# Second attention's loop: the next products are summed at the head of a step, the turns are spread over two steps

## The chip, the cores and the metric

One core of a Trainium2 chip runs the whole program in one launch. The metric is the device time of one execution in microseconds (us), lower is better. The kernel before takes 2010.0 us, the median of three runs.

## The reference, cut to what matters

Two layers, each an attention and a mixture of experts, over x of 8 x 512 tokens with 256 features. Only the second layer's attention, and what is loaded for the experts behind it, is touched.

```python
qkvw = x @ w_qkvw                      # x: 8 x 512 x 256
# sliced into q, k, v, w; 32 "batches" of 16 heads, head size 4, and the
# softmax runs over 16 heads' worth of positions, 16 x 16 scores at a time
attn = softmax(q @ k.T * 4 ** -0.5)
o = (attn @ v) * w @ w_out
x = x + gate * o
# then: layernorm, router (8 experts, the best one), gelu(x @ W1[e]) @ W2[e]
```

## The kernel before, in words

The program is written out by hand for five engines, each with its own list of instructions; semaphores are the only order between the lists, and each engine works strictly through its own list. All large tiles lie in one buffer, BIG, so the profile shows that name for nearly all of them.

The second attention runs as a loop of 64 steps q = 0 to 63; eight steps make a chunk c = q // 8. Step q of each engine's list:

- **GpSimd** (`products`, `values`): two products of q and k for step q + 2, into one of two buffers PB (128x1024, L1959); then half of the weighted values of step q (128x512, L1959), which waits for the exponentials of step q (`e_sb`). At steps 8c + 1 and 8c + 2 one pass of `finish` for the chunk before (128x1024).
- **VectorE** (`top`, `values`, `sums`): the maximum of the scores of step q + 1 (L1542), the weighted values of step q (L1111), the sums of step q - 1 (L1564), at every second step moments of an output tile (L1118), at the end of a chunk a reciprocal (L1567).
- **ScalarE** (`powers`, `powers_beside`): the exponentials of step q + 1 (L1880), copies of what TensorE projected or turned (L1618), the exponentials once more, into BIG (L1887), which sets `e_sb`.
- **TensorE**: `less_max(q + 1)` (waits for VectorE's maximum), at odd steps `out_project`, then the projections of a later chunk's heads (`project`, 16 for each chunk), the turns of its q and k (`turn_qk`, four for each chunk, each of four small transposing groups), at even steps `out_less`, then `scores(q + 2)`, which sums GpSimd's products (waits for `pm`), and at odd steps `out_turn`. The output tiles run in steps 13 to 61.

The heads of chunk c are projected in seven steps from 8c - 10 on (3, 3, 2, 2, 2, 2, 2), those of chunk 1 in steps 0 to 3 (4 each). All four turns of the next chunk stand in step 8c + 5. GpSimd can't start the products of a chunk before the four turned tiles are copied out of PSUM (`qt`).

SyncE's list issues the loads. The weights of the second layer's experts come in as 32 pieces of 512 KB (`weights_in(1, i)`, L499) whenever the part of BIG that they take is free: 4 behind chunk 4, 5 behind chunk 5, 6 after the last scores, 17 (`late`) later. Of these 15 are issued with every second of the rows that `rows_out` stores behind the loop, from row 3 on, and 2 after the last. `rows_out` stores each normalised row tile to HB (128 KB, L508) from a ring of four buffers; ScalarE waits for a store's landing before it fills the buffer again. TensorE reads the first piece only when all 32 have landed.

The router's weights are split into a high part (ScalarE) and a low part (VectorE) at tick 2 of that phase (`pre_tick`).

Of the kernel before, what the change touches and what calls it, by code (L numbers as in the profile page):

```python
# [8 lines left out]
ALU = mybir.AluOpType  # L9
# [59 lines left out]
def program(nc, x_in, wqk_in, wv_in, wo_in, rw_in, rb_in, w1_in, w3_in, w2_in, c0_in, m0_in,  # L69
# [3 lines left out]
    with ctx:  # L73
# [222 lines left out]
        def at(l, n):  # L296
            return per_layer[n] if l else 0
# [66 lines left out]
        def heads_by_step(c):  # L364
            if c == 1:
                return {0: 4, 1: 4, 2: 4, 3: 4}
            return {8 * c - 10 + n: k for n, k in enumerate((3, 3, 2, 2, 2, 2, 2))}

        heads_at = {q: [] for q in range(-10, 8 * 8)}
        for c in range(1, 8):  # L370
# [4 lines left out]

        def turns_next(q):

            return range(4) if q % 8 == 5 and q < 56 else ()

        NQ = 64  # L380
        N_IN = 24
# [51 lines left out]
        def sync(e):  # L433
# [136 lines left out]
            def out_weights_in(c):  # L570
                if c >= 6:
                    sp.wait_ge(s["pj_ps"], 128)
                elif c >= 2:
                    sp.wait_ge(s["pd_ps"], 4 * (c - 2) + 4)
                e.dma_start(out_weights(c).rearrange("p m k d -> p (m k d)"), WB[c]).then_inc(ld_wu[c % 2], 16)

            for c in range(7):
                heads_out(c)
                out_weights_in(c)
                for n in range(4 * c, 4 * c + 4):  # L580
                    out_in(n)
                if c == 1:
                    router_in(1)
                if c == 4:

                    sp.wait_ge(s["pj_ps"], 64)
                    for i in range(4):
                        weights_in(1, i)
                if c == 5:

                    sp.wait_ge(s["rl_ps"], 32)
                    sp.wait_ge(s["pj_ps"], 128)
                    sp.wait_ge(s["pm"], pm_p[55])
                    for i in (4, 5, 16, 17, 29):
                        weights_in(1, i)
            out_weights_in(7)
            sp.wait_ge(s["s_ps"], NQ)
            sp.wait_ge(s["pm"], pm_p[NQ - 1])
            for i in (12, 13, 14, 15, 19, 20):
# [7 lines left out]
            sp.wait_ge(s["mx_ps"], NQ)  # L607
            sp.wait_ge(s["pd_ps"], N_IN)
            sp.wait_ge(s["fin"], 16)
            late = [6, 7, 8, 9, 10, 11, 18, 21, 22, 23, 24, 25, 26, 27, 28, 30, 31]  # L610
            for n in range(3, NT):
                rows_out(1, n)
                if n % 2:
                    weights_in(1, late.pop(0))
            for i in late:
                weights_in(1, i)
# [13 lines left out]
        def tensor(e):  # L630
# [376 lines left out]
            def scores(q):  # L1007
                if q >= NQ:
                    return
                if pm_by(q).count("d"):  # L1010
                    pe.wait_ge(s["pm_d"], pm_v[q])
                pe.wait_ge(s["pm"], pm_p[q])
                if q >= 3:
                    pe.wait_ge(s["e_sb"], q - 2)
                else:
                    pe.wait_ge(s["cb_m"], NT)
                    pe.wait_ge(s["seld"], 4)
                for b in range(4):
                    m = mm(ps[2 + q % 3][32 * b:32 * b + 32, :], seld, PB[q % 2][:, b].rearrange("p r f -> p (r f)"), True, False)
                m.then_inc(s["s_ps"], 1)  # L1020

            def less_max(q):
                if q >= NQ:
                    return
                pe.wait_ge(s["sm"], q + 1)
                mm(shaped(ps[2 + q % 3][:, :], (2, 16, 16)), negid, bc(SM[q % 4], 3, 16), False, True).then_inc(s["mx_ps"], 1)
# [42 lines left out]
            less_max(0)  # L1069
            scores(1)  # L1070
            for q in range(NQ):
                less_max(q + 1)
                for n in out_at(q, O_OUT):
                    out_project(n)
                for c, h in heads_at[q]:
                    project(c, h)
                turn_qk(q // 8 + 1, turns_next(q))
                for n in out_at(q, O_LESS):
                    out_less(n)
                scores(q + 2)  # L1080
                for n in out_at(q, O_TURN):
                    out_turn(n)
            pe.wait_ge(s["e_sb"], NQ)
# [23 lines left out]
        def vector(e):  # L1107
            dve = Lane(e)

            def tt(o, a, b, op):  # L1110
                return e.tensor_tensor(o, a, b, op)  # L1111
# [167 lines left out]
            attended(NT - 1)  # L1279


            def pre_tick(l, t):
                m_ = M[l]
                for k, i in steps(NT, 7, t):
                    if k != 0:
                        continue
                    b = i // 4
                    if i == 2:
                        dve.wait_ge(s["rw_hi"], at(l, "rw_hi") + 1)
                        tt(m_.RW[1].rearrange(FLAT), m_.RWf.rearrange(FLAT), m_.RW[0].rearrange(FLAT), ALU.subtract).then_inc(s["rw_lo"], 1)  # L1290
                    o = at(l, "hr")
                    if l:
                        dve.wait_ge(s["rs_v"], (52, 54, 56)[max(b - 5, 0)])
                    else:
                        dve.wait_ge(s["rs_v"], 16 + 2 * b + 2)
                    dve.wait_ge(s["sc_ps"], at(l, "sc_ps") + b + 1)
                    if i >= 4:
                        dve.wait_ge(s["hs_lo"], at(l, "hs_lo") + i - 3)
                    h, sc = m_.HR[i % 4], ps[4 + b % 2]
                    x = row_tile(l, i)  # L1300
                    e.scalar_tensor_tensor(out=h, in0=X[:, x, :], scalar=stat[:, x, 0:1], in1=sc[:, 256:512],
                                           op0=ALU.subtract, op1=ALU.mult).then_inc(s["hr"], 1)
                    dve.wait_ge(s["hr"], o + 2 * i + 1)
                    e.scalar_tensor_tensor(out=h, in0=h, scalar=rstd[:, x:x + 1], in1=sc[:, 0:256],
                                           op0=ALU.mult, op1=ALU.add).then_inc(s["hr"], 1)
# [249 lines left out]
            def sums(q):  # L1555
                if q < 0:
                    return
                c, q2 = q // 8, q % 8
                dve.wait_ge(s["vm"], vm_n[q])
                dve.wait_ge(s["vm_p"], q + 1)  # L1560
                dve.wait_ge(s["e_sb"], q + 1)
                if q2 == 0 and c >= 2:
                    dve.wait_ge(s["fin"], 2 * (c - 2) + 1)
                e.tensor_reduce(OB[c % 2][:, 2 * q2:2 * q2 + 2], PV[q % 2], AX.X, ALU.add).then_inc(s["vr"], 1)  # L1564
                if q2 == 7:
                    dve.wait_ge(s["vr"], q + 1)
                    e.reciprocal(OB[c % 2][:, :, :, 4], OB[c % 2][:, :, :, 4]).then_inc(s["rcp"], 1)  # L1567

            def out_measure(n):
                dve.wait_ge(s["wx"], n + 1)  # L1570
                moments(3 * NT + n, out_tile(n))
# [4 lines left out]
            for q in range(NQ):  # L1576
                top(q + 1)
                values(q, 0)
                values(q, 1)
                sums(q - 1)  # L1580
                for n in out_at(q, O_MEASURE):
                    out_measure(n)
            sums(NQ - 1)

            def deviation(g):
# [28 lines left out]
        def scalar(e):  # L1614
# [104 lines left out]
            root(15, row(NT - 1))  # L1719


            def pre_tick(l, t):
                m_ = M[l]
                for k, i in steps(NT, 7, t):
                    if k == 5:
                        act.wait_ge(s["hT_ps"], at(l, "hT_ps") + i + 1)
                        if i >= 2:
                            act.wait_ge(s["lg_ps"], at(l, "lg_ps") + i - 1)
                        copy(m_.HTR[i % 2], bank16(6 + i % 2)).then_inc(s["hT"], 1)
                    if k == 2:  # L1730
                        act.wait_ge(s["hr"], at(l, "hr") + 2 * i + 2)
                        if i >= 4:
                            act.wait_ge(st_hb[i % 4], slot_base[l]["hb"] + 16 * (i // 4))
                            act.wait_ge(s["hT_ps"], at(l, "hT_ps") + i - 3)
                        copy(m_.HP[i % 4][:, 0, :], m_.HR[i % 4]).then_inc(s["hs_hi"], 1)
                    if k == 0 and i == 2:
                        act.wait_ge(ld_r, slot_base[l]["r"] + 32)
                        copy(m_.RW[0].rearrange(FLAT), m_.RWf.rearrange(FLAT)).then_inc(s["rw_hi"], 1)

            def routing(l):  # L1740
                m_ = M[l]
# [168 lines left out]
            for q in range(NQ):  # L1910
                powers(q + 1)
                for n in out_at(q, O_OUT):
                    out_x(n)
                for n in out_at(q - 1, O_TURN):
                    out_hi(n)
                for c, h in heads_at[q]:
                    project(c, h)
                turn_qk(q // 8 + 1, turns_next(q))
                for n in out_at(q, O_LESS):
                    out_lo(n)  # L1920
                powers_beside(q + 1)

            def late_root(g):
# [271 lines left out]
```

## Time and profile before

| | |
|---|---|
| median of three runs | 2010.0 us (2005.67 to 2013.35) |
| the profiled execution | 2012.52 us, its span 2010.4 us |
| mean granted TensorE clock | 0.893 of full |
| loop of the second attention | about 1211 to 1639 us of the span |
| rows stored, routing | about 1639 to 1712 us |
| experts and the end | about 1712 to 2010 us |
| busy share of the span | TensorE 85%, VectorE 57%, GpSimd 52%, ScalarE 43% |

A row of the timeline gives the start and length in us of one instruction, or of several in a row of one kind (x26: 26 of them), with the time that the engine was idle before it and the work that released it. GpSimd is POOL, VectorE DVE, ScalarE ACT, TensorE PE (its weight loads PEld), SyncE SP. The clock column of a stretch is the granted clock as a share of 2.4 GHz. An idle engine matters only where it is the one that others wait for.

### The profile page before, as it was taken

The page shows a single profiled execution, that of the slowest core. Times are in us where ns is not written, and L with a number is a line of the kernel's source. Part 1 is how long each engine was busy: PE and PEld are TensorE (multiplying, and loading weights), DVE is VectorE, ACT ScalarE, POOL GpSimd, SP SyncE. Part 2 cuts the span into 40 slices and gives each one's busy share as a digit, 9 for nine tenths or more (in the row PEclk, how much of TensorE's full clock was granted, in tenths as well). Part 3 has the DMA queues.
Part 4 walks back from the last instruction along what each step waited for, and adds up shares of the span by engine and source line. Part 5 has one row for each costly group of instructions (what it writes and reads, how often), then busy time and mean ns, then how long its engine had stood idle before and what let it go on. Part 6 is the DMA issues. An engine that isn't in the chain of part 4 may idle for free.

```text
span 2010.4 us, 32271 instructions
## 1 busy us (share of the span) xinstructions
PE 1715.6 (85%) x11144; PEld 1040.9 (52%) x11144; DVE 1141.3 (57%) x1837; ACT 866.5 (43%) x1940; POOL 1047.0 (52%) x861
## 2 busy tenths in 40 slices
PE   5699999977899999999999367788887766899993
PEld 3355555554466666666666232334333234577771
DVE  6798898866232332332333685888888886212124
ACT  3444444334344444444444374344444335444443
POOL 3377777623233333333443697989888853233322
PEclk8699999975899999999999678899889876899996
DMA  5013332007322332222443510011102147111115
GB/s 210 1 42 105 105 105 99 28 32 281 107 82 84 93 95 92 90 79 88 129 137 85 165 43 1 22 27 27 27 25 69 65 138 235 35 43 43 43 39 174
DMA packets 114358, 170.47 MB, mean 85 GB/s; under 512 B 27920, under 2 KB 78112, under 8 KB 114080
## 3 DMA queue, kind: packets, MB, share of 16 engines
q1 hardware_dynamic: 104032, 140.61, 20.6%
q0 software_dynamic: 10176, 27.80, 5.3%
q8 instruction: 102, 1.67, 0.4%
q14 instruction: 48, 0.39, 0.1%
HBM read 105.19 MB, written 63.18 MB: 84 GB/s over the span
## 4 chain that ended last, share of the span: by engine, by line
PE 69%; DVE 19%; issue 3%; DMA 3%; ACT 3%; POOL 2%; SPq 0%; DVEq 0%; POOLq 0%; ACTq 0%
PE ps L634 62%; DVE BIG L1111 8%; PE ps L905 5%; DVE BIG L1564 4%; ACT BIG L1618 1%; PE ps L877 1%; DVE bnst L1118 1%; DVE BIG L1542 1%; DMA BIG<-YT 1%; DVE X L1111 1%; POOL BIG L2072 1%; PE ps L809 1%; PE ps L749 1%; DMA HB<-BIG 1%; POOL X L1959 1%
## 5 line engine op out<-in xcount | busy, mean ns | idle before, releaser
L634 PE MATMUL ps<-BIG 128*128 (+8 forms) x8100 | 1318.0, 340 | 150.8 <-DVE BIG L1542 78.3
L634 PEld LDWEIGHTS ps<-BIG 128*128 128x128 f16 (+2 forms) x8100 | 746.2, 105 | 633.8 <-issue 137.4
L1959 POOL TENSOR_TENSOR BIG<-BIG 128x512 f16<-128x512 f32 (+4 forms) x528 | 763.1, 1474 | 309.7 <-ACT BIG L1618 287.7
L1618 ACT ACTIVATE BIG<-ps 128x512 f16<-128x512 f32 (+5 forms) x1036 | 397.6, 441 | 518.6 <-PE ps L634 270.6
L1111 DVE TENSOR_TENSOR BIG<-ps,BIG 128x512 f32<-128x512 f32 (+4 forms) x693 | 460.8, 718 | 272.8 <-ACT BIG L1618 225.8
L2046 POOL DMA_INDIRECT YT<-BIG x106 | 105.1, 992 | 542.2 <-ACT BIG L1618 542.2
L1111 DVE TENSOR_TENSOR BIG<-BIG,ps 128x512 f32<-128x512 f32 (+1 forms) x204 | 120.9, 597 | 413.6 <-PE ps L634 398.4
L1618 ACT ACTIVATE BIG<-BIG 128x512 f16<-128x512 f32 (+2 forms) x329 | 200.4, 626 | 130.7 <-DVE BIG L1111 98.8
L1769 ACT ACTIVATE BIG<-ps 128x512 f32<-128x512 f32 x212 | 126.8, 598 | 135.7 <-PE ps L634 135.7
L1564 DVE TENSOR_REDUCE BIG<-BIG 128x160 f32<-128x2560 f32 x64 | 180.8, 2826 | 0.0
L2041 POOL DMA_INDIRECT BIG<-HB,BIG x106 | 103.2, 973 | 69.8 <-DVE BIG L1111 43.8
L905 PE MATMUL ps<-ident,BIG 128*128 128x128 f32 x848 | 109.9, 273 | 0.0
L905 PEld LDWEIGHTS ps<-ident,BIG 128*128 128x128 f32 x848 | 99.2, 141 | 20.1
L1880 ACT ACTIVATE ps<-ps 128x512 f32<-128x512 f32 x64 | 37.2, 582 | 137.6 <-PE ps L634 137.6
L1111 DVE TENSOR_TENSOR BIG<-BIG 128x1024 f32<-128x1024 f32 (+16 forms) x115 | 80.9, 727 | 17.6 <-ACT BIG L1618 14.3
L1542 DVE TENSOR_REDUCE BIG<-ps 128x32 f32<-128x512 f32 x64 | 43.7, 682 | 79.3 <-PE ps L634 79.3
L634 PE MATMUL ps<-MOD,sel 8*128 8x256 f32 (+1 forms) x96 | 55.8, 703 | 27.5 <-DVE BIG L1111 15.7
L634 PE MATMUL ps<-BIG,tri 128*128 128x512 f16 x260 | 64.2, 389 | 5.1 <-DVE BIG L1111 5.1
L1118 DVE BATCH_NORM_STATS2 bnst<-X 128x6 f32<-128x256 f32 x128 | 53.9, 421 | 8.0 <-DMA X<-in_x 3.3
L1887 ACT ACTIVATE BIG<-ps 128x512 f32<-128x512 f32 x64 | 38.5, 602 | 37.9 <-DVE BIG L1564 37.8
L877 PEld LDWEIGHTS ps<-ident,BIG 128*128 128x128 f16 x424 | 32.7, 99 | 36.8 <-issue 12.4
L877 PE MATMUL ps<-ident,BIG 128*128 128x128 f16 x424 | 41.6, 221 | 11.1 <-DMA BIG<-HB,BIG 11.1
(128 smaller groups left out, 864.7 us busy)
## 6 DMA issues: line engine op xcount, KB each, us to landing
WD<-BIG SPq DMA_DIRECT2D x112, 256.0 KB, 2.3
BIG<-in_v SPq DMA_DIRECT2D x32, 512.0 KB, 5.1
BIG<-WD SPq DMA_DIRECT2D x32, 512.0 KB, 5.1
BIG<-in_w SPq DMA_DIRECT2D x24, 512.0 KB, 3.9
BIG<-WD SPq DMA_DIRECT2D x32, 384.0 KB, 7.5
BIG<-YT SPq DMA_DIRECT2D x24, 512.0 KB, 4.8
HB<-BIG SPq DMA_DIRECT2D x64, 128.0 KB, 3.0
X<-in_x SPq DMA_DIRECT2D x4, 1024.0 KB, 12.1
```

Source lines behind the costliest of these rows:

```text
L634: return e.matmul(o, lhsT, rhs, start=start, stop=stop, skip_group_check=True)
L877: m = e.transpose(bank16(6 + idx % 2)[:, k, :], m_.HIN[j % 3][:, k * 128:(k + 1) * 128], ident16[:, :])
L905: m = e.transpose(ps[6 + (2 + 3 * j + q) % 2][:, n * 128:(n + 1) * 128], m_.UP[j % 2][:, (4 * q + n) * 128:(4 * q + n + 1) * 128], ident[: ...
L1111: return e.tensor_tensor(o, a, b, op)
L1118: e.bn_stats(bnst[:, r, :], X[:, i, :]).then_inc(s["bn"], 1)
L1542: e.tensor_reduce(SM[q % 4], shaped(ps[2 + q % 3][:, :], (2, 16, 16)), AX.X, ALU.max).then_inc(s["sm"], 1)
L1564: e.tensor_reduce(OB[c % 2][:, 2 * q2:2 * q2 + 2], PV[q % 2], AX.X, ALU.add).then_inc(s["vr"], 1)
L1618: return e.activation(o, i, ACT.Copy)
L1769: e.activation(m_.UP[j % 2][:, hf * 512:hf * 512 + 512], ps[idx % 4][:, :], ACT.Silu if m_.gated else ACT.Gelu).then_inc(s["su"], 1)
L1959: return e.tensor_tensor(o, a, b, op)
L2041: e.indirect_dma_start(m_.HIN[j % 3], None, m_.HB, bass.IndirectOffsetOnAxis(m_.gi[:, j:j + 1], 0)).then_inc(ld_hi[j % 3], 16)
L2046: e.indirect_dma_start(m_.YT, bass.IndirectOffsetOnAxis(m_.yi[:, j:j + 1], 0), m_.YO[j % 2], None).then_inc(st_y[j % 2], 16)
```

## The change

- `scores(q + 2)` moves from behind `out_less` to the head of TensorE's step q, ahead of `less_max(q + 1)`.
- The heads of a chunk are projected in six steps instead of seven (3, 3, 3, 3, 2, 2), and the four turns are spread over steps 8c + 4 (two) and 8c + 5 (two).
- Pieces 8 and 11 of the second layer's expert weights are issued behind chunk 5, pieces 6 and 9 before the last scores; `late` holds 13 pieces, and one is issued with every fourth row instead of every second (8 with rows, 5 after the last).
- The router's weights of the second layer are split inside the loop: the high part at ScalarE's step 40, the low part at VectorE's step 42.

```diff
         def heads_by_step(c):
             if c == 1:
                 return {0: 4, 1: 4, 2: 4, 3: 4}
-            return {8 * c - 10 + n: k for n, k in enumerate((3, 3, 2, 2, 2, 2, 2))}
+            return {8 * c - 10 + n: k for n, k in enumerate((3, 3, 3, 3, 2, 2))}
...
         def turns_next(q):
-            return range(4) if q % 8 == 5 and q < 56 else ()
+            return {4: (0, 1), 5: (2, 3)}.get(q % 8, ()) if q < 56 else ()
...
                     sp.wait_ge(s["pm"], pm_p[55])
-                    for i in (4, 5, 16, 17, 29):
+                    sp.wait_ge(s["fin"], 12)
+                    for i in (4, 5, 16, 17, 29, 8, 11):
                         weights_in(1, i)
             out_weights_in(7)
+            sp.wait_ge(s["vm"], vm_n[55])
+            sp.wait_ge(s["vm_p"], 56)
+            for i in (6, 9):
+                weights_in(1, i)
...
-            late = [6, 7, 8, 9, 10, 11, 18, 21, 22, 23, 24, 25, 26, 27, 28, 30, 31]
+            late = [7, 10, 18, 21, 22, 23, 24, 25, 26, 27, 28, 30, 31]
             for n in range(3, NT):
                 rows_out(1, n)
-                if n % 2:
+                if n % 4 == 3:
                     weights_in(1, late.pop(0))
...
             for q in range(NQ):
+                scores(q + 2)
                 less_max(q + 1)
                 for n in out_at(q, O_OUT):
                     out_project(n)
...
                 for n in out_at(q, O_LESS):
                     out_less(n)
-                scores(q + 2)
                 for n in out_at(q, O_TURN):
                     out_turn(n)
...
+            def router_lo(l):
+                m_ = M[l]
+                dve.wait_ge(s["rw_hi"], at(l, "rw_hi") + 1)
+                tt(m_.RW[1].rearrange(FLAT), m_.RWf.rearrange(FLAT), m_.RW[0].rearrange(FLAT), ALU.subtract).then_inc(s["rw_lo"], 1)
...
                     out_measure(n)
+                if q == 42:
+                    router_lo(1)
...
+            def router_hi(l):
+                act.wait_ge(ld_r, slot_base[l]["r"] + 32)
+                copy(M[l].RW[0].rearrange(FLAT), M[l].RWf.rearrange(FLAT)).then_inc(s["rw_hi"], 1)
...
                     out_lo(n)
+                if q == 40:
+                    router_hi(1)
                 powers_beside(q + 1)
```

## Rows read from the trace of the kernel before

**Rows 1.** The page: shares of the chain that ended last, by engine.
```profile
PE 69%; DVE 19%; issue 3%; DMA 3%; ACT 3%; POOL 2%; SPq 0%; DVEq 0%; POOLq 0%; ACTq 0%
```

**Rows 2.** Busy time of two stretches of eight steps (us, instructions, TensorE's clock, DMA).
```profile
1255.70:1304.80 49.10, 37.05 (x209) 14.52 (x209) 42.67 (x34) 19.73 (x68) 45.91 (x27) 0.88 0.09 22
1358.40:1413.00 54.60, 44.26 (x261) 20.94 (x262) 44.75 (x41) 23.15 (x81) 46.28 (x27) 0.91 0.10 25
```

**Rows 3.** Waits in steps 6 to 61: total us, times, longest.
```profile
DVE BIG L1542 <- PE ps L634: 61.8, 27, 5.1
POOL BIG L1959 <- ACT BIG L1618: 48.2, 7, 8.3
...
POOL BIG L1959 <- ACT BIG L1887: 8.2, 9, 2.4
```

**Rows 4.** Timeline of GpSimd: start, us, work, idle before it and its releaser.
```profile
1254.48 45.90 POOL L1959 TENSOR_TENSOR BIG<-BIG 128x1024 f32<-128x1024 f32 x26 [6.31 <-ACT BIG L1618]
...
1303.57 26.49 POOL L1959 TENSOR_TENSOR BIG<-BIG 128x1024 f32<-128x1024 f32 x15 [3.19 <-ACT BIG L1618]
...
1395.23 7.22 POOL L1959 TENSOR_TENSOR BIG<-BIG 128x1024 f32<-128x1024 f32 x4
1402.92 1.28 POOL L1959 TENSOR_TENSOR BIG<-BIG 128x512 f32<-128x512 f32 x1 [0.47 <-ACT BIG L1887]
...
1412.05 26.51 POOL L1959 TENSOR_TENSOR BIG<-BIG 128x1024 f32<-128x1024 f32 x15 [7.84 <-ACT BIG L1618]
1439.13 17.88 POOL L1959 TENSOR_TENSOR BIG<-BIG 128x512 f32<-128x512 f32 x10 [0.57 <-ACT BIG L1887]
...
1576.24 46.57 POOL L1959 TENSOR_TENSOR BIG<-BIG 128x1024 f32<-128x1024 f32 x26 [7.97 <-ACT BIG L1618]
```

**Rows 5.** Timeline of step 29, the turns of four.
```profile
1402.68 0.67 DVE L1542 TENSOR_REDUCE BIG<-ps 128x32 f32<-128x512 f32 x1
...
1403.41 1.78 PE L634 MATMUL ps<-BIG 128*128 128x512 f32 x8 [2.05 <-DVE BIG L1542]
...
1405.55 2.40 PE L634 MATMUL ps<-BIG,ident 32*32 32x512 f32 x16
...
1407.83 1.24 ACT L1618 ACTIVATE BIG<-ps 128x512 f32<-128x512 f32 x2 [1.58 <-PE ps L634]
```

**Rows 6.** Timeline of steps 30 and 31, three heads each.
```profile
1413.78 3.32 PE L634 MATMUL ps<-BIG 128*128 128x512 f32 x20 [0.18 <-DVE BIG L1542]
...
1417.14 1.06 PE L634 MATMUL ps<-BIG 128*32 128x512 f32 x8
...
1419.37 1.78 PE L634 MATMUL ps<-BIG 128*128 128x512 f32 x8 [1.17 <-DVE BIG L1542]
...
1424.09 0.62 ACT L1887 ACTIVATE BIG<-ps 128x512 f32<-128x512 f32 x1
```

**Rows 7.** Busy time and clock of short stretches, after waits of various length.
```profile
1273.30:1279.80 6.50, 6.40 (x22) 2.52 (x22) 4.42 (x4) 2.09 (x8) 6.50 (x5) 0.52 0.01 4
1280.50:1284.00 3.50, 3.43 (x22) 1.63 (x22) 3.50 (x3) 1.60 (x7) 3.50 (x3) 1.00 0.00 0
...
1378.20:1382.00 3.80, 3.80 (x11) 1.94 (x12) 3.80 (x3) 0.58 (x1) 3.80 (x3) 0.55 0.00 0
```

**Rows 8.** Timeline: the last maximum of the loop.
```profile
1625.31 0.69 DVE L1542 TENSOR_REDUCE BIG<-ps 128x32 f32<-128x512 f32 x1 [1.11 <-PE ps L634]
```

**Rows 9.** Waits behind the loop, ScalarE's for the row buffers.
```profile
ACT BIG L1618 <- DMA HB<-BIG: 5.2, 5, 1.4
```

**Rows 10.** Busy time while the last rows are stored.
```profile
1680.00:1694.40 14.40, 10.76 (x118) 6.84 (x118) 6.61 (x15) 9.66 (x22) 7.67 (x15) 0.50 0.95 312
```

**Rows 11.** Timeline of SyncE's queue: pieces of the weights.
```profile
1589.31 2.29 SPq L499 DMA_DIRECT2D BIG<-WD  x5
...
1693.48 1.47 SPq L499 DMA_DIRECT2D BIG<-WD  x3
```

**Rows 12.** Chain of waits: the first products with those weights.
```profile
1717.33 5.32 PE ps L634 x12
```

More of the change, by code:

```diff
@@ L1287, in pre_tick @@
                     b = i // 4
-                    if i == 2:
-                        dve.wait_ge(s["rw_hi"], at(l, "rw_hi") + 1)
-                        tt(m_.RW[1].rearrange(FLAT), m_.RWf.rearrange(FLAT), m_.RW[0].rearrange(FLAT), ALU.subtract).then_inc(s["rw_lo"], 1)
+                    if l == 0 and i == 2:
+                        router_lo(0)
                     o = at(l, "hr")
@@ L1735, in pre_tick @@
                         copy(m_.HP[i % 4][:, 0, :], m_.HR[i % 4]).then_inc(s["hs_hi"], 1)
-                    if k == 0 and i == 2:
-                        act.wait_ge(ld_r, slot_base[l]["r"] + 32)
-                        copy(m_.RW[0].rearrange(FLAT), m_.RWf.rearrange(FLAT)).then_inc(s["rw_hi"], 1)
+                    if l == 0 and k == 0 and i == 2:
+                        router_hi(0)
             def routing(l):
```

## The prediction

> **What bounds the kernel now.** I read the page's chain first: it ends on TensorE for 69% and on VectorE for 19% [rows 1]. That is an average over stages, so I cut the second attention's loop into its eight-step chunks. There no engine is full: in 54.6 us TensorE is busy 44.3, VectorE 44.8, GpSimd 46.3 [rows 2]. The waits say that VectorE stands 61.8 us for TensorE's sums before a maximum, and GpSimd 48.2 us, seven times, for ScalarE [rows 3]. The first is what the move of `scores` would take away. The second decides how much of it can be kept. GpSimd's timeline shows it working 45.9 us without a gap, 26 instructions, the work of a chunk, and then standing 3.2 to 8 us for the turned tiles; outside that it waits only 0.47 and 0.57 us [rows 4]. So a chunk lasts 45.9 us plus GpSimd's idle time: 46.57 + 7.97 = 54.5, for instance. However early the maxima come, time is gained only where GpSimd idles less. Its price by piece, from the same rows: two products 4.0 us, values 1.25, so a step takes it 5.25 us.
>
> **The turn, before and after.** Let t = 0 be the end of GpSimd's last products of a chunk, 1395.23 + 7.22 = 1402.45. Before, the next products start at 1412.05, 9.6 us later [rows 4], because the turns wait for `less_max` and `out_project` (1403.41 to 1405.55, 2.14 us) and are then four [rows 5]. After the change TensorE at step 8c + 5 must first sum the very products that end at t = 0: 1.06 us [rows 6], 1.2 with issue. Then 2.14 for `less_max` and `out_project`, then two turns: 2.28 from their start to the first copy (1405.55 to 1407.83) and 1.24 for two copies [rows 5]. That is 6.9, GpSimd starts at 7.0: **2.6 us less** for a chunk. The other two turns stand in step 8c + 4, which has no heads any more: 1.2 + 0.55 + 2.4 + 0.3 = 4.5 us against GpSimd's 5.25, hidden.
>
> **What it gives back.** The moved sum is a new wait: TensorE stops at the head of step 8c + 6 until the first products of the new chunk are there, at 7.0 + 4.0 = 11.0, while it was free at 1.2 + 2.14 + 2.4 + 0.7 = 6.45. Behind that wait stand `less_max(8c + 7)`, three heads and, through ScalarE's copies, the second exponentials for which GpSimd's values wait. It is 4.5 us idle, and rows show the clock after such waits at 0.52 and 0.55, the 1.2 GHz level; the same 22 matmuls then took 6.40 instead of 3.43 us, the other stretch cost 3.8 x 0.45 = 1.7 us of work [rows 7]. I take 2.3 us, between 1.7 and 3.0, and bound it below by none. Step 8c + 6 then takes 1.06 + 3.36 [rows 6] + 2.3 = 6.6, to 17.6, with copies and exponentials to 18.5. GpSimd is ready at 11.0 + 1.25 + 4.0 = 16.25: it waits **2.25 us** (0 at full clock, 3 at most).
>
> In step 8c + 7, odd with three heads, the exponentials start 4.72 us after `less_max` starts (1419.37 to 1424.09 [rows 6]) and last 0.6; with the sum ahead of them they are done 6.5 us after the products, where GpSimd comes back after 5.25. Counted from 17.9 they end at 24.3, GpSimd is ready at 23.8: **0.5 us**, and 1.3 to 1.5 if step 8c + 6 ran at full clock. In step 8c + 11 (two heads, 0.8 less) it is 5.7 against 5.25: **0.5 us**. In steps 8c + 9 and 8c + 10 `finish` gives GpSimd 2 us of other work, which covers them. Sum 3.25 us; the 0.47 and 0.57 of before go. Per chunk: -2.6 + 3.25 - 1.04 = **-0.4 us** (from -2.0 at full clock to +0.8), five chunks: **-2.0 us**.
>
> **The other chunks.** The turn in step 5: GpSimd idled 6.31 us before 1254.48. The new way to the turned tiles has no `out_project`, 1.2 + 0.55 + 3.5 = 5.3 us after its products, 2.8 us earlier. But in steps 0 to 3, with four heads, the second exponentials come 1.2 + 0.55 + 3.3 + 0.9 = 5.95 us after the products, 0.6 to 0.7 late, in about two steps. Net **-1.7**. The turn in step 13: idle before 3.19 [rows 4], after 5.4 - 1.25 = 4.1, and then the 2.25 of the low clock: **+3.2** (from +0.9). The last chunk has no turn behind it and no heads: from the products at 1576.24 eight pairs, seven values and two passes of `finish`, 32 + 8.8 + 4 = 44.8, and 1.2 to the last maximum, against 1625.31 - 1576.24 = 49.07 before [rows 4, 8]: **-3.0**. The loop: -1.7 + 3.2 - 2.0 - 3.0 = **-3.5 us**.
>
> **The weights and the router.** Behind the loop ScalarE waits 5.2 us in all for the ring's stores to land [rows 9], at a DMA share of 0.95 while the last rows go out [rows 10]. Half of the pieces among the rows are gone. I take 2.3 of the 5.2 us, as part of the waits lies beside TensorE's late output tiles; bounds 0 and 5.2. Now five pieces instead of three are issued at the end, near 1694 [rows 11]. At the 312 GB/s of that stretch five are 8.5 us, landed near 1703; the weights are first used at 1717.3 [rows 12], so they cost nothing, and would from 14 us more. The four pieces moved into the loop go where SyncE stood still anyway: 8 and 11 behind the five at 1589 [rows 11], ahead of a store of the heads that GpSimd hasn't finished by then; 6 and 9 behind that store. Their new waits (`fin` 12, `vm`, `vm_p` of step 55) ask for what the stores of the heads before them in SyncE's list have already waited for, so nothing queues up behind them. The router's two small instructions fill gaps on VectorE and ScalarE in the loop: -0.2 behind it. Tail **-2.5 us**.
>
> **Sum.** -3.5 - 2.5 = -6.0 us on the profiled execution, 2012.5 to 2006.5. That execution lies 2.5 above the median of the runs, 2010.0, so the forecast is **2004 us**.
>
> **Rivals.** (C) *GpSimd's waits outside the turn vanish*, because the clock holds and the steps after a turn fit beside 5.25 us. Then a chunk is 45.9 + 5.7 = 51.6, so -3.6 x 5 = -18; with -1.7 + 0.9 - 3.0 and -3 in the tail -25 us, 1985. For it: TensorE has only 44 us of work in a chunk, some of it at low clock; against it the odd steps with three heads, 6.5 us. (B) *All is given back*: 4.3 us of waits in a chunk and a tail limited by TensorE's late tiles. -2.6 + 4.3 - 1.04 = +0.66 a chunk, +3.3 for five in place of -2.0, tail -0.2: +1.6, about 2011.5. (D) *Slower: step 8c + 7 runs at the low clock too.* Its 5.5 us become 5.5 x 1.87 = 10.3 (the ratio of 6.40 to 3.43 [rows 7]), 4.8 us more wait of GpSimd in each of five chunks, +24: 2028. It decides from 3.2 us a chunk on. Against it: the stretch behind the low one, after a wait of only 0.8 us, is back at 1.00. The Trainium skill ("TensorE: Matmul & The Clock Gate", section "Why this matters for your kernels") has a rule against this change: waiting gaps between bursts of matmuls put the clock back to its lower level. Taken for step 8c + 6 alone it gives the forecast, taken for every waiting step it gives D. The rows agree for the long waits, not for those of 0.8 us.
>
> **Chances.** The forecast (about 1999 to 2008) 0.50, B 0.20, C 0.17, D 0.13. What a measurement here can tell from no change is about 0.5%, 10 us. Faster by more: C and a third of the forecast's band, 0.33. Slower by more: D and the edge of B, 0.16. The rest 0.51. The range from 1989 to 2016 takes in the low clock from none to full on step 8c + 6, a tail from 0 to 5.2 and half of C, and leaves out D and C's far end.
>
> **What would show it.** VectorE's 61.8 us of waits for sums shrink or move to other places, and TensorE waits for GpSimd at the heads, about 4.5 us once in a chunk. GpSimd's waits before new products fall from 7.9 to about 5.7 us, and new ones of 1 to 3 us for L1887 appear in the two steps after. A low clock stands behind each such wait. Chunks of 54 to 54.5 us confirm the sum, of 52 C, of 58 D. The prediction is wrong if GpSimd is no longer the fullest engine of a chunk, or if stores to HB still hold ScalarE for 5 us.

## The result: slower by 0.9%, and the profile after

The changed kernel takes 2027.6 us, the median of five runs (2026.08 to 2031.96), against 2010.2 of the kernel before, measured with it: a ratio of 1.0088 with an interval of 1.0068 to 1.0108. The forecast was 2004, with a range up to 2016; the measurement lies outside it. The profiled execution took 2026.8 us, its span 2024.7, 14.3 more than before. In the changed kernel's rows VectorE's maximum is L1551, its weighted values L1116, GpSimd's products and values L1975, ScalarE's two exponentials L1894 and L1901, its copies L1629, TensorE L639.

The page, the shares of the chain by engine, as [rows 1]:

```profile
PE 63%; POOL 14%; DVE 10%; issue 6%; DMA 3%; ACT 3%; SPq 0%; POOLq 0%; DVEq 0%; ACTq 0%
```

Before, the chain ended on TensorE and VectorE, with 2% for GpSimd; now GpSimd holds 14% of it and VectorE 10%. A chunk of eight steps, as [rows 2] (length, busy us of TensorE, its weight loads, VectorE, ScalarE, GpSimd, the clock, DMA):

```profile
1358.10:1416.30 58.20, 44.44 (x260) 20.60 (x260) 45.47 (x42) 22.58 (x81) 46.08 (x27) 0.88 0.10 24
```

The work is the same, 44.4 us of TensorE and 46.1 of GpSimd, and the chunk lasts 58.2 us where it lasted 54.6. The waits in the same stretch, from the first turn to the last maximum (total us, times, longest), as [rows 3]:

```profile
PE ps L639 <- POOL BIG L1975: 94.2, 41, 4.6
DVE BIG L1551 <- PE ps L639: 42.8, 15, 4.7
POOL BIG L1975 <- ACT BIG L1901: 38.3, 21, 3.2
DVE BIG L1116 <- ACT ps L1894: 37.1, 27, 1.9
...
POOL BIG L1975 <- ACT BIG L1629: 29.7, 6, 5.7
```

VectorE's wait for sums fell from 61.8 to 42.8 us, but 37.1 us of waits for the first exponentials appeared behind it. TensorE, which waited 1.2 us for GpSimd before, does it 41 times, 94.2 us. GpSimd's wait for the turned tiles is 29.7 us in six turns here; with the turn of step 5, whose 3.46 us lie just ahead of this stretch, it is 33.1 in seven, against 48.2 in seven before. Its wait for the second exponentials rose from 8.2 to 38.3: what the turns gave is more than given back. Where, GpSimd's timeline shows, as [rows 4]: the start of a chunk in steps 6 and 14, one whole chunk (steps 30 to 37), and the last one.

```profile
1248.65 9.11 POOL L1975 TENSOR_TENSOR BIG<-BIG 128x1024 f32<-128x1024 f32 x5 [3.46 <-ACT BIG L1629]
...
1301.50 9.12 POOL L1975 TENSOR_TENSOR BIG<-BIG 128x1024 f32<-128x1024 f32 x5 [2.47 <-ACT BIG L1629]
...
1416.27 9.11 POOL L1975 TENSOR_TENSOR BIG<-BIG 128x1024 f32<-128x1024 f32 x5 [5.24 <-ACT BIG L1629]
1428.18 10.39 POOL L1975 TENSOR_TENSOR BIG<-BIG 128x512 f32<-128x512 f32 x6 [2.80 <-ACT BIG L1901]
1439.15 19.73 POOL L1975 TENSOR_TENSOR BIG<-BIG 128x512 f32<-128x512 f32 x11 [0.58 <-ACT BIG L1901]
1462.03 6.70 POOL L1975 TENSOR_TENSOR BIG<-BIG 128x512 f32<-128x512 f32 x4 [3.14 <-ACT BIG L1901]
1474.13 2.00 POOL L1975 TENSOR_TENSOR BIG<-BIG 128x1024 f32<-128x1024 f32 x1 [5.39 <-ACT BIG L1629]
...
1590.27 9.11 POOL L1975 TENSOR_TENSOR BIG<-BIG 128x1024 f32<-128x1024 f32 x5 [5.41 <-ACT BIG L1629]
```

From the first products of a chunk to the next: 52.85 us for the one with the turn of step 13 (49.09 before), then 56.6, 58.2, 57.9, 58.5 and 57.7, where it was 54.5, 54.0, 54.7, 55.0 and 54.5. The five together are 16.1 us longer. In the chunk shown GpSimd idles 5.24 us for the turns, 2.80 behind step 8c + 6, 0.58, and **3.14 us at 1462.03**, behind step 8c + 11 (here 35), where the forecast had 0.5. The critical chain through this place (start, length, work; x3: three instructions):

```profile
1447.45 6.30 POOL BIG L1975 x3
1453.75 0.04 issue
1453.79 7.14 PE ps L639 x30
...
1461.46 0.50 ACT BIG L1901
1461.96 0.07 issue
1462.03 0.95 POOL BIG L1975
```

Read it forward. GpSimd's products for TensorE's head of step 35 end at 1453.75. TensorE sums them at once and works through the step for 7.14 us; only then come ScalarE's second exponentials, and GpSimd's next values start at 1462.03. TensorE's own rows at the heads of steps 34 and 35, and the clock of four stretches, as [rows 7]: step 30's head, step 34, the wait after it, step 35.

```profile
1446.29 3.43 PE L639 MATMUL ps<-BIG 128*32 128x512 f32 x22 [1.93 <-POOL BIG L1975]
...
1453.79 5.22 PE L639 MATMUL ps<-BIG 128*32 128x512 f32 x16 [3.96 <-POOL BIG L1975]
```

```profile
1420.30:1426.80 6.50, 6.50 (x29) 2.80 (x29) 2.62 (x4) 1.89 (x8) 5.08 (x3) 0.63 0.00 0
1446.30:1449.70 3.40, 3.40 (x23) 1.72 (x23) 2.40 (x5) 1.25 (x5) 3.40 (x2) 1.00 0.00 0
1449.90:1453.70 3.80, 0.00 (x0) 0.00 (x0) 3.72 (x3) 1.14 (x5) 3.80 (x3) 0.83 0.76 155
1453.80:1459.00 5.20, 5.20 (x17) 2.01 (x18) 1.31 (x2) 0.58 (x1) 5.09 (x3) 0.50 0.19 60
```

Step 34 is over in 3.4 us at the full clock. Then TensorE does nothing for 3.96 us, and the first 5.2 us of step 35 run at 0.50, the 1.2 GHz level; its last 2.3 us show 0.95. The 6.5 us at 0.63 at 1420.3 are the low stretch that was forecast; the one at 1453.8 was not. The same happens in the last chunk (TensorE's last sum, and, as [rows 8], the last maximum):

```profile
1637.07 4.22 PE L639 MATMUL ps<-BIG 128*32 128x512 f32 x16 [1.70 <-POOL BIG L1975]
```

```profile
1639.58 0.68 DVE L1551 TENSOR_REDUCE BIG<-ps 128x32 f32<-128x512 f32 x1
```

Sixteen matmuls take 4.22 us there, and 2.78 us at the full clock elsewhere; the last maximum starts 49.31 us after the chunk's first products (1639.58 minus 1590.27), against 49.07 before. Behind the loop ScalarE's waits for the row buffers went from 5.2 to 4.4 us, as [rows 9]:

```profile
ACT BIG L1629 <- DMA HB<-BIG: 4.4, 4, 2.4
```

So the 14.3 us are: -5.8 up to the first chunk's products (1254.48 to 1248.65; 1.75 of them were already there before the loop, where the code is the same), +3.8 for the chunk of step 13, +16.1 for five chunks, +0.2 for the last, +1.1 from the last maximum to `finish` and -1.1 from there to the end.

### The profile page after: what moved, and what is told of

It reads as the page before. It is cut to its first block, busy times and chain, and to the rows that moved or that the text cites. A ratio compares the mean times of both kernels' runs of the same rounds, so it can differ in the third digit from the quotient of the medians.

```text
span 2024.7 us, 32272 instructions
## 1 busy us (share of the span) xinstructions
PE 1710.4 (84%) x11144; PEld 1034.7 (51%) x11144; DVE 1143.0 (56%) x1837; ACT 862.9 (43%) x1940; POOL 1048.9 (52%) x861
## 4 chain that ended last, share of the span: by engine, by line
PE 63%; POOL 14%; DVE 10%; issue 6%; DMA 3%; ACT 3%; SPq 0%; POOLq 0%; DVEq 0%; ACTq 0%
PE ps L639 56%; POOL BIG L1975 13%; DVE BIG L1116 5%; PE ps L910 5%; ACT BIG L1629 1%; PE ps L882 1%; DMA BIG<-YT 1%; POOL BIG L2088 1%; DVE X L1116 1%; DMA HB<-BIG 1%; DVE bnst L1123 1%; POOL X L1975 1%; PE ps L814 1%; PE ps L754 1%; DMA BIG<-in_m 0%
## 5 line engine op out<-in xcount | busy, mean ns | idle before, releaser
L639 PE MATMUL ps<-BIG 128*128 (+9 forms) x8100 | 1320.6, 342 | 175.0 <-POOL BIG L1975 114.2
L639 PEld LDWEIGHTS ps<-BIG 128*128 128x128 f16 (+2 forms) x8100 | 742.9, 105 | 669.9 <-issue 173.1
L1975 POOL TENSOR_TENSOR BIG<-BIG 128x512 f16<-128x512 f32 (+4 forms) x528 | 764.9, 1473 | 323.6 <-ACT BIG L1629 270.8
L1116 DVE TENSOR_TENSOR BIG<-ps,BIG 128x512 f32<-128x512 f32 (+4 forms) x693 | 462.5, 724 | 311.3 <-ACT BIG L1629 224.7
L1629 ACT ACTIVATE BIG<-ps 128x512 f16<-128x512 f32 (+5 forms) x1036 | 397.5, 439 | 511.1 <-PE ps L639 264.8
L1116 DVE TENSOR_TENSOR BIG<-BIG,ps 128x512 f32<-128x512 f32 (+1 forms) x204 | 121.0, 597 | 413.5 <-PE ps L639 398.2
L1629 ACT ACTIVATE BIG<-BIG 128x512 f16<-128x512 f32 (+2 forms) x329 | 200.6, 626 | 129.6 <-DVE BIG L1116 98.2
L1783 ACT ACTIVATE BIG<-ps 128x512 f32<-128x512 f32 x212 | 127.0, 599 | 134.5 <-PE ps L639 134.5
L1894 ACT ACTIVATE ps<-ps 128x512 f32<-128x512 f32 x64 | 37.2, 582 | 204.9 <-PE ps L639 204.9
L910 PE MATMUL ps<-ident,BIG 128*128 128x128 f32 x848 | 109.9, 273 | 0.0
L1116 DVE TENSOR_TENSOR BIG<-BIG 128x1024 f32<-128x1024 f32 (+16 forms) x115 | 80.7, 725 | 13.3 <-ACT BIG L1629 10.0
L639 PE MATMUL ps<-MOD,sel 8*128 8x256 f32 (+1 forms) x96 | 55.8, 704 | 28.0 <-DVE BIG L1116 16.2
L1551 DVE TENSOR_REDUCE BIG<-ps 128x32 f32<-128x512 f32 x64 | 43.7, 683 | 52.0 <-PE ps L639 51.8
L639 PE MATMUL ps<-BIG,tri 128*128 128x512 f16 x260 | 63.5, 386 | 4.5 <-DVE BIG L1116 4.5
L976 PE MATMUL ps<-ident,BIG 128*128 128x128 f32 x64 | 17.9, 382 | 36.0 <-DVE BIG L1140 18.3
```

Source lines behind the costliest of these rows:

```text
L639: return e.matmul(o, lhsT, rhs, start=start, stop=stop, skip_group_check=True)
L910: m = e.transpose(ps[6 + (2 + 3 * j + q) % 2][:, n * 128:(n + 1) * 128], m_.UP[j % 2][:, (4 * q + n) * 128:(4 * q + n + 1) * 128], ident[: ...
L1551: e.tensor_reduce(SM[q % 4], shaped(ps[2 + q % 3][:, :], (2, 16, 16)), AX.X, ALU.max).then_inc(s["sm"], 1)
L1629: return e.activation(o, i, ACT.Copy)
L1783: e.activation(m_.UP[j % 2][:, hf * 512:hf * 512 + 512], ps[idx % 4][:, :], ACT.Silu if m_.gated else ACT.Gelu).then_inc(s["su"], 1)
```

## The experiments

Each ratio is to the kernel before on the same chip, with its 95% interval. "After" is the changed kernel. The kernel before was measured again with each group of kernels (medians 2008.1 to 2010.2), so a difference of 2 us between medians of different groups says little. The kernels compute the whole reference unless it is said otherwise.

### One part at a time

`a1_sum_last` is after with the sum where it was:

```diff
             for q in range(NQ):
-                scores(q + 2)
                 less_max(q + 1)
...
                     out_less(n)
+                scores(q + 2)
                 for n in out_at(q, O_TURN):
```

> The changed kernel with scores(q + 2) back behind out_less; heads, turns, weights and router stay changed. If the moved sum is the cause (TensorE waits at the head of a step for GpSimd's products), the chunks of 58 us fall below the 54.5 of before, since the turned tiles still come some 3 us earlier: 1985 to 2003 us. If the heads in six steps or the split turns are the cause, it stays at 2020 or more.

Measured: 1989.7 us (1985.03 to 1991.48), 0.9908 (0.9884 to 0.9932). `a2_sum_first_only` is before with only the opposite edit, the sum at the head.

> The kernel before with nothing changed but scores(q + 2) at the head of the step. If the moved sum is the cause: as slow as the changed kernel or slower, since all four turns now stand behind the wait for the last products (about 3 us more in a chunk): 2030 to 2050 us. If heads and turns are the cause: about 2010.

Measured: 2045.3 us (2042.72 to 2050.32), 1.0188 (1.0161 to 1.0214). One chunk and the next's start in GpSimd's timeline:

```profile
1424.65 9.11 POOL L1959 TENSOR_TENSOR BIG<-BIG 128x1024 f32<-128x1024 f32 x5 [10.13 <-ACT BIG L1618]
1437.09 30.11 POOL L1959 TENSOR_TENSOR BIG<-BIG 128x512 f32<-128x512 f32 x17 [3.33 <-ACT BIG L1887]
1469.37 6.44 POOL L1959 TENSOR_TENSOR BIG<-BIG 128x512 f32<-128x512 f32 x4 [2.16 <-ACT BIG L1887]
1486.14 9.10 POOL L1959 TENSOR_TENSOR BIG<-BIG 128x1024 f32<-128x1024 f32 x5 [10.34 <-ACT BIG L1618]
```

The chunk lasts 61.5 us. All four turns still stand in step 8c + 5, now with the sum ahead of them, so the turn's idle time is 10.1 us, 2.3 more than in [rows 4], and two waits of 3.33 and 2.16 us stand behind it. `b3_turns_only` is before with only the heads in six steps and the turns in two:

```diff
-            return {8 * c - 10 + n: k for n, k in enumerate((3, 3, 2, 2, 2, 2, 2))}
+            return {8 * c - 10 + n: k for n, k in enumerate((3, 3, 3, 3, 2, 2))}
...
-            return range(4) if q % 8 == 5 and q < 56 else ()
+            return {4: (0, 1), 5: (2, 3)}.get(q % 8, ()) if q < 56 else ()
```

> The kernel before with the heads in six steps and the turns in steps 4 and 5, and nothing else of the change. If the gain of the run with the sum put back is the turns' (GpSimd's idle time at a turn 3 us shorter, six times): 1989 to 1994 us. If it needs the weights' new spread too: 2000 or more.

Measured: 1989.1 us (1988.36 to 1989.8), 0.9904 (0.9883 to 0.9924). Its GpSimd:

```profile
1448.14 26.52 POOL L1959 TENSOR_TENSOR BIG<-BIG 128x1024 f32<-128x1024 f32 x15 [4.69 <-ACT BIG L1618]
1476.31 19.64 POOL L1959 TENSOR_TENSOR BIG<-BIG 128x512 f32<-128x512 f32 x11 [1.64 <-ACT BIG L1887]
1499.71 20.74 POOL L1959 TENSOR_TENSOR BIG<-BIG 128x1024 f32<-128x1024 f32 x12 [3.77 <-ACT BIG L1618]
```

The turn's wait falls to 4.69 and 3.77 us without any move of the sum, less than the 5.24 of after, one wait of 1.64 is left in a chunk, and a chunk lasts 51.6 us. So the parts add up: the sum at the head costs 37 us (before to `a2`) or 38 (`a1` to after), spreading the turns gains 19 (before to `b3`). The gain never needed the move. These three came out inside the first of the ranges expected for them.

`a3_weights_as_before` is after with the weights' pieces issued as before (`late` of 17 pieces, every second row, none moved into the loop).

> The changed kernel with the weights' pieces issued as before. Prediction's tail term: 2.3 us for ScalarE's waits for the row buffers, so 2028 to 2032 against the changed kernel's 2027.6. If the pieces moved into the loop or left for the end cost time: below 2025.

Measured: 2029.7 us (2029.14 to 2034.7), 1.0117 (1.0095 to 1.014), 2.1 above after; the two intervals overlap. In the profiled executions it takes 372.5 us from `finish` to the end against 370.5, and ScalarE waits 6.0 us for row buffers against 4.4.

### Is it the clock or the order?

`a4_keep_busy` is after with idle matmuls on TensorE, 34 behind the turned tiles of step 8c + 5 and 30 at the end of step 8c + 2, into a bank that holds nothing at that time. It adds work that nothing reads; the output's computation stays.

```diff
+            def keep_busy(q):
+                if q % 8 == 2 and 8 < q < 64:
+                    ...
+                    for _ in range(30):
+                        mm(ps[0][:, 256:384], ones[:, :], tri[:, :], True, True)
+                if q % 8 == 5 and q < 56:
+                    pe.wait_ge(s["qt"], 4 * (q // 8 + 1) + 4)
+                    for _ in range(34):
+                        mm(ps[0][:, 256:384], ones[:, :], tri[:, :], True, True)
...
                     out_turn(n)
+                keep_busy(q)
```

> The changed kernel with idle matmuls (f16, 128 columns, into an unused half bank) where TensorE waits longest: 34 behind the copies of the turned tiles in step 8c + 5, 30 at the end of step 8c + 2; they add no result. If the low clock behind the waits is what delays the exponentials, GpSimd's waits of 2.9 and 3.1 us in a chunk fall to about 0.7 each and the clock there is full: 2000 to 2010 us. If it is the order alone, the sum of 1.2 us ahead of less_max: 2023 to 2030.

Measured: 2013.1 us (2003.22 to 2017.06, ten runs), 1.0013 (0.9994 to 1.0031). The clock of step 35 and of the turn's step after it; then TensorE's idle matmuls and the sum behind them, and GpSimd behind step 35 and at the next chunk's start:

```profile
1450.90:1456.00 5.10, 4.97 (x34) 3.04 (x34) 2.93 (x4) 1.93 (x9) 5.10 (x4) 1.00 0.21 68
1462.30:1466.50 4.20, 4.20 (x17) 1.81 (x18) 3.19 (x3) 0.88 (x2) 1.27 (x1) 0.63 0.01 4
```

```profile
1447.52 1.85 PE L639 MATMUL ps<-tri,ones 128*128 128x128 f16 x30 [0.49 <-ACT BIG L1643]
1450.99 2.78 PE L639 MATMUL ps<-BIG 128*32 128x512 f32 x16 [1.62 <-POOL BIG L1989]
...
1456.62 5.59 POOL L1989 TENSOR_TENSOR BIG<-BIG 128x512 f32<-128x512 f32 x3 [0.53 <-ACT BIG L1915]
...
1470.45 9.12 POOL L1989 TENSOR_TENSOR BIG<-BIG 128x1024 f32<-128x1024 f32 x5 [6.50 <-ACT BIG L1643]
```

The 30 matmuls take 1.85 us of a wait of 3.96. Step 35 then runs at 1.00, and GpSimd's wait behind it is 0.53 us instead of 3.14. Behind the turn the fill helped less, 2.12 us instead of 2.80. In this chunk the low clock, no longer in step 35, stands in step 37 (1462.3, 0.63), where the last turns' exit is due, and GpSimd waits 6.50 us for them instead of 5.39. Even so the median falls by 14.5 us, to between the two ranges that were expected. In step 35 the clock was nearly the whole wait: with it at 1.00 the 3.14 us are 0.53, the 0.5 of the prediction. Of the 38 us that the sum at the head costs in all, 23 are left (`a4` against `a1`), and this run doesn't split them between the order and the low clock that remains.

`b1_weigh_later` leaves TensorE's list alone and shifts GpSimd's `weigh` pass by one step, so that the products for the head of step 8c + 11 come 2 us earlier:

```diff
-                if q % 8 == 2 and q > 8:
+                if q % 8 == 3 and q > 8:
                     finish(q // 8 - 1, "weigh")
```

> The changed kernel with GpSimd's second pass of finish one step later (8c + 3 instead of 8c + 2), nothing else. Theory: the two passes of 2 us fall before the products of two steps running, so TensorE, which now waits at the head, stands 3.96 us at step 8c + 11 and runs that odd step at 1.2 GHz; GpSimd loses 3.1 us there. Apart, neither wait is longer than about 2.3 us, the clock stays up and the 3.1 become 0.5: 2010 to 2016 us. Rival, the place of finish is indifferent and only the order counts: 2024 to 2030.

Measured: 2015.1 us (2012.13 to 2020.76, ten runs), 1.0029 (1.0015 to 1.0043). One pass at another place gives 12.5 us, within the 2010 to 2016 expected. `d1_weigh_later_router_back` is the same with the router's two instructions behind the loop again.

> The changed kernel with GpSimd's second pass of finish one step later, and the router's instructions behind the loop. In the run with the pass alone (2015.1 us) one VectorE instruction of 128x16 took 11.3 us. If the low clock at step 8c + 11 cost what the traces say (3.1 down to 0.5 us of GpSimd's wait, six chunks) and that instruction cost the rest of the run, this gives 2003 to 2009 us. If the instruction was hidden: 2013 to 2017.

Measured: 2013.3 us (2012.24 to 2018.48, six runs), 1.0025 (1.0011 to 1.0039), the case in which the instruction was hidden. Its TensorE at the heads of steps 35 and 36, and GpSimd at the end of the chunk:

```profile
1448.03 2.78 PE L639 MATMUL ps<-BIG 128*32 128x512 f32 x16 [1.66 <-POOL BIG L1971]
...
1455.53 3.94 PE L639 MATMUL ps<-BIG 128*32 128x512 f32 x10 [2.53 <-POOL BIG L1971]
...
1463.70 1.27 POOL L1971 TENSOR_TENSOR BIG<-BIG 128x512 f32<-128x512 f32 x1 [2.83 <-ACT BIG L1899]
1468.45 9.11 POOL L1971 TENSOR_TENSOR BIG<-BIG 128x1024 f32<-128x1024 f32 x5 [3.48 <-ACT BIG L1627]
```

TensorE waits 1.66 us at the head of step 35 and its 16 matmuls take 2.78 us, full clock. The delay stands one step on: 2.53 us at the head of step 36, whose ten take 3.94 instead of 2.12 us. GpSimd waits 2.83 us before the last values and only 3.48 for the turns. A chunk lasts 55.2 us.

`b2_max_then_sum` is after with the two lines at the head swapped, `less_max(q + 1)` first, then `scores(q + 2)`; the heads and the output tile stay behind the wait.

> The changed kernel with less_max(q + 1) first and scores(q + 2) directly behind it. If all that harms is that less_max stands behind the wait (first exponentials late): back to 2005 or less. If what harms is the heads and output tile behind the wait, through ScalarE's copies to the second exponentials, that stays: 2015 to 2027.

Measured: 1999.3 us (1997.24 to 2001.86), 0.9949 (0.9931 to 0.9967). That is the first of the two cases: most of the harm was that `less_max` stood behind the wait, not that heads and output tile do. GpSimd:

```profile
1403.39 9.12 POOL L1975 TENSOR_TENSOR BIG<-BIG 128x1024 f32<-128x1024 f32 x5 [4.42 <-ACT BIG L1629]
1414.63 30.08 POOL L1975 TENSOR_TENSOR BIG<-BIG 128x512 f32<-128x512 f32 x17 [2.13 <-ACT BIG L1901]
...
1457.02 9.12 POOL L1975 TENSOR_TENSOR BIG<-BIG 128x1024 f32<-128x1024 f32 x5 [4.54 <-ACT BIG L1629]
```

A chunk is 53.6 us; the largest wait outside the turn is 2.13 us. TensorE still waits 4.03 us in step 8c + 11 and the clock still falls there, to 0.72, but the maximum's matmuls, on which the rest of the step hangs, are ahead of the wait. That place is worth 28 of the 38 us. The low clock costs less here, but not nothing: GpSimd still waits 1.20 us (at 1445.91) for the exponentials of that step, and `c2` below removes it.

### VectorE's small instruction

In `b1` the router's low part, 16 columns on VectorE in the middle of the loop, shows another cost. The rows are the instruction, GpSimd behind it, and the same instruction in after:

```profile
1495.80 11.29 DVE L1116 TENSOR_TENSOR BIG<-BIG 128x16 f16<-128x16 f32 x1
```

```profile
1515.10 5.36 POOL L1975 TENSOR_TENSOR BIG<-BIG 128x512 f32<-128x512 f32 x3 [8.03 <-ACT BIG L1901]
```

```profile
1505.19 0.36 DVE L1116 TENSOR_TENSOR BIG<-BIG 128x16 f16<-128x16 f32 x1
```

It reads two SBUF tiles, started while GpSimd was in a block of 19.72 us (from 1487.35) and ended at 1507.09, when that block ended (1507.07). The second exponentials came late, and GpSimd waited 8.03 us. In `b2` the same took 11.19 us, in `a1`, `b4` and `a4` 1.99 to 2.15, in after 0.36: the change had put it there and I had priced it at nothing. After's 0.36 us stood in the middle of a GpSimd block too (1497.19 to 1516.93), so the block alone doesn't decide it. `c1_max_then_sum_router_back` is `b2` with both router instructions back behind the loop.

> The changed kernel with less_max ahead of scores, and the router's two small instructions back behind the loop. In the run with that order alone (1999.3 us) VectorE's instruction of 128x16 took 11.2 us, until GpSimd paused. If that wait lay on the path, this is 6 to 10 us faster: 1989 to 1993. If it was hidden: 1998 to 2001.

Measured: 1994.2 us (1992.83 to 2000.11), 0.9932 (0.9909 to 0.9954), 5.1 below `b2` and between the two ranges expected. The chunk that holds the instruction, from its first products at 1457.02 in `b2` to the next, takes 59.3 us with it and 54.2 in `c1`, where it starts at 1456.77. From `b1` to `d1` the same edit gave 1.8 us only, though there that chunk went from 63.5 to 53.8 us. In both pairs the intervals overlap. `c2_both_moves` adds the later `weigh` to `c1`.

> As the run before it, with GpSimd's second pass of finish one step later too. If the low clock at step 8c + 11 still costs there (1.2 us of GpSimd's time in a chunk), 4 to 6 us less than it: 1984 to 1988. If GpSimd's turn waits take it back: the same.

Measured: 1985.0 us (1982.88 to 1986.08), 0.9881 (0.9856 to 0.9906), 9.1 below `c1`. So with `less_max` first the place of the pass still counts: GpSimd works 36.55 us on without a gap (from 1410.18), and a chunk takes 51.4 us instead of 53.6.

### Towards the fastest version

`b4_turns_earlier` has the sum last, a later chunk's heads as 4, 3, 3, 3, 3 (chunk 1: 6, 5, 5) and the turns in steps 8c + 3 and 8c + 4.

> The changed kernel with the sum back at the end, heads of a chunk in five steps (4, 3, 3, 3, 3; chunk 1: 6, 5, 5 in steps 0 to 2) and the turns in steps 3 and 4. If GpSimd's 45.9 us bound a chunk and it stands only for the turned tiles, the 3 to 5 us of idle go: 1965 to 1980 us. If TensorE's odd steps bound the chunk by then: 1985 or more.

Measured: 1984.1 us (1980.07 to 1988.46), 0.9874 (0.9846 to 0.9902), above the 1965 to 1980 expected. The waits at the turn are gone, but GpSimd now waits 3.3 to 3.5 us once in most chunks for the second exponentials (3.46 us at 1428.74). `c3_balanced` is `b4` with the router's instructions behind the loop and fewer heads in the odd steps, which carry `out_project`:

```diff
-            return {8 * c - 10 + n: k for n, k in enumerate((4, 3, 3, 3, 3))}
+            return {8 * c - 10 + n: k for n, k in enumerate((4, 2, 4, 2, 4))}
```

> Sum at the end, turns in steps 3 and 4 (1984.1 us with heads 4, 3, 3, 3, 3), heads now 4, 2, 4, 2, 4 with the short odd ones beside the output tiles, router's instructions behind the loop. If TensorE's odd steps hold the chunk: 1970 to 1980. If GpSimd's work (45.9 us a chunk) does: 1981 to 1985.

Measured: **1969.2 us** (1964.34 to 1972.34), 0.98 (0.9771 to 0.9829), the fastest. A chunk of its loop, and GpSimd:

```profile
1410.10:1458.80 48.70, 41.67 (x260) 19.78 (x260) 45.30 (x42) 22.94 (x80) 46.29 (x26) 0.96 0.11 28
```

```profile
1410.08 7.08 POOL L1971 TENSOR_TENSOR BIG<-BIG 128x512 f32<-128x512 f32 x4 [0.39 <-ACT BIG L1899]
1418.20 18.35 POOL L1971 TENSOR_TENSOR BIG<-BIG 128x512 f32<-128x512 f32 x10 [1.03 <-ACT BIG L1899]
...
1458.89 40.75 POOL L1971 TENSOR_TENSOR BIG<-BIG 128x512 f32<-128x512 f32 x23 [0.37 <-ACT BIG L1899]
...
1505.63 7.08 POOL L1971 TENSOR_TENSOR BIG<-BIG 128x512 f32<-128x512 f32 x4 [0.38 <-ACT BIG L1899]
```

GpSimd's longest wait here is 1.03 us; the two chunks from 1410.08 to 1505.63 take 95.55 us, 47.8 each, against 46 of GpSimd's own work, and the clock is 0.96. `c4_earlier_weigh_later` (`b4`, router back, `weigh` one step later) and `d2_balanced_weigh_later` (`c3` with the later `weigh`) ask whether that pass still matters.

> Sum at the end, turns in steps 3 and 4, heads 4, 3, 3, 3, 3, router's instructions behind the loop, GpSimd's second pass of finish one step later. TensorE doesn't wait for the products at the head there, so the place of finish should not matter: 1981 to 1985. If it falls below 1978, finish costs in this order too.

> The fastest run so far (sum last, turns in steps 3 and 4, heads 4, 2, 4, 2, 4, router's instructions behind the loop: 1969.2 us) with GpSimd's second pass of finish one step later. If the last pass of finish still holds products for which TensorE waits: 1962 to 1967. If GpSimd is full by now: the same, 1967 to 1971.

Measured: 1974.7 us (1974.19 to 1977.68), 0.983 (0.9806 to 0.9853), and 1969.3 us (1968.39 to 1969.94), 0.9805 (0.9789 to 0.9822). `d2` equals `c3`: where GpSimd has hardly a gap, its order gives nothing. `c4` is 9.5 below `b4`, by the pass and the router together, and below the 1978 that was to show that the pass costs in this order too; the two weren't separated there, so that isn't shown. `c4` and `d2` differ in the heads alone: 4, 2, 4, 2, 4 instead of 4, 3, 3, 3, 3 takes 5.4 us off the median (the intervals overlap) and GpSimd's one wait in a chunk from 3.38 us (at 1419.31 in `c4`) to 1.23 (at 1413.74 in `d2`). The rest of the 14.9 us from `b4` to `c3` isn't the heads' alone.

## Why the prediction was wrong, step by step

- **The turn: right.** Forecast 5.7 us of idle time instead of 7.9; measured 5.24 to 5.69 in five turns. But it was credited to a change of two edits. `b3` shows that the spread turns alone give it and more, 3.5 to 4.7 us of idle time: with the sum at the head, 1.2 us by the forecast, the turn pays for products that it doesn't need.
- **A slip in the sum.** The 2.6 us saved at the turn run from 1402.45 to 1412.05 and so hold the 0.47 us wait of before, which the 1.04 takes off once more. Without that a chunk comes to +0.1 instead of -0.4, 2.4 us in five chunks. Rivals B and C carry the same slip; C's own chunk of 51.6 is 2.9 us below 54.5, not 3.6. It isn't what made the forecast fail.
- **Behind the turn: nearly right.** Step 8c + 6 at a low clock, 2.25 us forecast, 2.80 measured. The 0.5 us of step 8c + 7 didn't come; a wait of 0.58 stands one step later, ahead of the values of step 33, behind TensorE's step 32.
- **Step 8c + 11: the step that failed.** The prediction priced it at 0.5 us and said of steps 8c + 9 and 8c + 10: "`finish` gives GpSimd 2 us of other work, which covers them". It covers GpSimd's own waits. But the same 2 us delay the products for TensorE's next heads, and the change had just made TensorE wait for these. After the short step 34 it stood 3.96 us, most of step 35 ran at 1.2 GHz, and GpSimd paid 3.14 us. I followed GpSimd's work in these steps only as cover, not as a supplier. `a4` shows that at this place the cost is the clock (0.53 us with it held up), `b1` and `d1` that the pass is what makes the gap.
- **The five chunks in sum.** Over the five chunks from 1301.50 to 1590.27 GpSimd's rows, less those of before, give: turns -11.54, behind step 8c + 6 +13.51, behind 8c + 8 +3.00, behind 8c + 11 +14.78, the small waits of before -5.53, its own work +1.88, together +16.10 us where the forecast had -2.0. The 14.78 of step 8c + 11 stand against 2.5 forecast: 12.3 of the 18.1 us by which the five chunks missed, and the 18.1 are most of the 20.3 us between the forecast and the measured profiled execution.
- **Rival D had the mechanism at another place.** It let step 8c + 7 run low and gave 2028; that step ran at 1.00 (1426.8 to 1432.6), behind step 8c + 6 without a wait of TensorE, and an odd step behind a long wait elsewhere paid. I weighed it against waits of 0.8 us alone, without asking which of the other heads would wait longer. "Chunks of 58: D" is the sign that came true. That D's 2028 is so near the 2027.6 measured is luck: its 4.8 us a chunk stood at a step that cost nothing.
- **The start and step 13: signs right.** Forecast -1.7 and +3.2, measured -4.1 (beyond the 1.75 that were there before) and +3.8. The start gained more than twice its forecast.
- **The last chunk: wrong sign.** -3.0 forecast, +0.2 measured. The sum of GpSimd's work up to the last products, 44.8 us, was nearly right (44.4), but two waits of 1.19 us stand in it and the last sum ran at the low level, 2.5 us to the maximum instead of 1.2. The same cause again: without heads TensorE waits 1.7 to 4.6 us ahead of most of its sums (4.12 us ahead of 1625.53).
- **The weights and the tail.** For the weights 2.3 us were forecast; `a3` gives 2.1 by the medians and 2.0 in its profile, which agrees but is no sharper than the runs. The whole tail was forecast at -2.5 us and gave nothing: +1.1 from the last maximum to `finish`, -1.1 from there on. Stores to HB held ScalarE for 4.4 us instead of 5.2, where 2.9 were forecast. The router's instructions, priced at nothing in the loop, are no gain: `b3` has neither them nor the new spread of the weights and equals `a1` (1989.1 and 1989.7), which has both, so by this estimate they take about what the weights give.

**Open.** Why moving the router's instruction gives 5.1 us in one order and 1.8 in another by the medians isn't settled, nor what sets its length. The profiles of `b1` and `d1` are already 3.5 us apart at the products of step 14 (1299.43 and 1302.89), where their code is the same. The 3.9 us by which `d1` is still above before are made of its waits behind steps 8c + 6 and 8c + 12; that is read from its timeline, not tested alone.

## What to carry to other kernels

Let an in-order engine do first what others wait for in this step, and last what is needed only for the next but one: moving a sum that is used two steps later to the head of the step cost 37 us here, though at its old place TensorE had waited only 1.2 us for the products in steps 6 to 61. Where a move makes engine A wait for engine B, list everything that B does between the products in each step of the period, rare passes too: what was cover for B becomes delay for A. And price a wait on TensorE with the clock of the work behind it, above all where a short step is followed by a long one; even out the steps too (2 and 4 heads instead of 3 and 3 took 5.4 us off, `c4` to `d2`).

## What the hardware showed

Behind a wait of 3.96 us the following 5.2 us of matmuls ran wholly at 0.50; with 1.85 us of idle matmuls in it, the same step ran at 1.00. Filling wasn't a cure, though: in that chunk the low clock then turned up two steps later, at 0.63. The length of the last wait alone doesn't tell what comes: waits of 1.66 us (1448.03 in `d1`) and 1.93 us (1446.29 in after) had the full clock behind them, one of 1.70 us in after's last chunk and one of 1.38 us in `a4`, ahead of 1462.27, a low one, the latter though TensorE had been busy 4.78 of the 6.3 us before it, at 1.00. The rows don't explain that one.

A VectorE subtraction of 16 columns with both inputs in SBUF took 0.36 to 11.3 us beside GpSimd. In `b1` its end and that of GpSimd's block are 0.02 us apart, in `b2` 0.04 (1497.28 and 1497.24). The Trainium skill ("Trainium Architecture — The Big Picture", section "What this means for kernel authors") says that the port pair shared by VectorE and GpSimd is locked by one of them and not split in bandwidth. The two long cases agree with that, and add that the small instruction can wait over 10 us, through several of GpSimd's. That the lock is the cause is not shown: no run took GpSimd away, and after's 0.36 us inside a block doesn't follow from it.
